# First stage of a vision-transformer kernel reordered: eight embed pieces, norm rows spread by a product, k ahead of q

## The reference

```
x = einsum('bchpwq,dcpq->bhwd', patches, conv_w)      # contraction over 32*8*8 = 2048
x = x.reshape(b, 256, 128) + conv_b
for i in range(2):
    y = _ln(x, ln1_g[i], ln1_b[i])                    # (x - mean) * rsqrt(var + eps) * g + b
    q, k, v = split(y @ qkv_w[i])                     # 8 heads of 64
    q = softmax(q, axis=-1) * scale                   # over a head's 64 columns
    k = softmax(k, axis=-2)                           # over the 256 tokens
    ctx = einsum('bhnd,bhne->bhde', k, v)
    x = x + einsum('bhnd,bhde->bhne', q, ctx) ... @ out_w[i] + out_b[i]
    ...                                               # layernorm, gelu network
```

## Time and profile before

| | |
|---|---|
| median of 3 runs | 131.5 us (131.13 to 131.67) |
| the profiled execution | 131.33 us, of which its span is 129.5 us |
| busy share of the span | PE 92%, PEld 80%, DVE 59%, ACT 50%, POOL 38% |
| DMA | 12.18 MB, nearly all in the first 34 us |
| granted TensorE clock | 1.000 over the span |

### The profile page before, as it was taken

How to read it: one execution, slowest core, us unless ns; L and a number is a source line. 1 busy time by engine, 2 the same in 40 slices (tenths; PEclk the granted TensorE clock), 3 DMA queues, 4 the chain that set the end, 5 groups by cost and what they waited for, 6 DMA issues and landing times.

```text
span 129.5 us, 2185 instructions
## 1 busy us (share of the span) xinstructions
PE 118.7 (92%) x820; PEld 103.5 (80%) x820; DVE 76.2 (59%) x239; ACT 64.3 (50%) x153; POOL 48.7 (38%) x60
## 2 busy tenths in 40 slices
PE   6999959999999999898999999669889988999991
PEld 6999958986987889796876989658578777998991
DVE  6000284897677945669999876347678478065002
ACT  3000153835397395467773649733772835423520
POOL 0000024034797575416759356086409123022000
PEclk9999999999999999999999999999999999999999
DMA  4999899999100000000000000000000000000101
GB/s 109 364 424 418 244 432 384 339 416 407 74 0 0 0 3 0 5 0 0 0 0 0 5 0 3 0 0 0 8 0 0 0 0 0 5 0 0 61 0 61
DMA packets 3884, 12.18 MB, mean 94 GB/s; under 512 B 441, under 2 KB 1817, under 8 KB 3618
## 3 DMA queue, kind: packets, MB, share of 16 engines
q1 hardware_dynamic: 3874, 12.05, 24.8%
HBM read 11.65 MB, written 0.39 MB: 93 GB/s over the span
## 4 chain that ended last, share of the span: by engine, by line
PE 65%; DVE 9%; DMA 9%; ACT 8%; SPq 3%; issue 3%; POOL 2%; DVEq 0%; ACTq 0%; POOLq 0%
DMA norm_rows_sb<-in_norm_rows 9%; PE bank L499 6%; PE bank L375 5%; PE bank L394 5%; PE bank L413 4%; PE bank L319 4%; PE bank L388 3%; PE bank L382 3%; PE bank L340 3%; PE bank L352 3%; SPq L261 3%; PE bank L365 3%; PE bank L485 2%; PE bank L401 2%; PE bank L370 2%
## 5 line engine op out<-in xcount | busy, mean ns | idle before, releaser
L1787 POOL TENSOR_TENSOR rstd<-mv,minus_half 128x2 f32<-128x2 f32 x14 | 10.0, 714 | 39.5 <-DVE mv L934 39.1
L1805 POOL TENSOR_TENSOR qn<-q,rqsum 128x512 f32<-128x512 f32 x8 | 8.3, 1044 | 12.7 <-DVE rqsum L994 12.7
L1566 ACT ACTIVATE patches_sb<-bank,fcb 128x256 f32<-128x256 f32 x12 | 5.1, 471 | 10.5 <-PE bank L496 10.5
L1525 ACT ACTIVATE kexp<-bank,nkmax 128x256 f32<-128x256 f32 x16 | 7.4, 470 | 5.7 <-DVE nkmax L974 5.7
L413 PE MATMUL bank<-restw,hid 128*128 128x128 f32 x64 | 8.8, 281 | 1.0 <-ACT hid L1540 1.0
L394 PEld LDWEIGHTS bank<-cw,qT 128*128 128x128 f32 x64 | 8.1, 191 | 1.7 <-issue 1.0
L499 PE MATMUL bank<-projw,patches_sb 128*128 128x192 f32 x48 | 9.4, 331 | 0.0
L394 PE MATMUL bank<-cw,qT 128*128 128x128 f32 x64 | 9.0, 285 | 0.1
L413 PEld LDWEIGHTS bank<-restw,hid 128*128 128x128 f32 x64 | 7.8, 191 | 1.6 <-ACT hid L1540 1.4
L319 PE MATMUL bank<-embed_sb 128*128 128x128 f32 x64 | 8.5, 288 | 0.0
L319 PEld LDWEIGHTS bank<-embed_sb 128*128 128x128 f32 x64 | 8.1, 200 | 0.3 <-DMA embed_sb<-in_embed 0.2
(11 more groups left out here) (168 smaller groups left out, 341.4 us busy)
## 6 DMA issues: line engine op xcount, KB each, us to landing
embed_sb<-in_embed SPq DMA_DIRECT2D x3, 768.0 KB, 6.9
patches_sb<-in_patches SPq DMA_DIRECT2D x2, 1024.0 KB, 12.5
restw<-in_rest_w SPq DMA_DIRECT2D x2, 768.0 KB, 16.7
qkvw<-in_qkv_w SPq DMA_DIRECT2D x3, 256.0 KB, 11.7
qkvw<-in_qkv_w SPq DMA_DIRECT2D x1, 768.0 KB, 16.5
fcw<-in_fc_w SPq DMA_DIRECT2D x1, 768.0 KB, 18.4
embed_sb<-in_embed SPq DMA_DIRECT2D x1, 576.0 KB, 4.1
aqkvw<-in_aqkv_w SPq DMA_DIRECT2D x1, 576.0 KB, 12.8
```

The costliest lines, as they stand in the source:

```text
L1525: return nc.scalar.activation(kexp[:, c, :], K_BANK[s][c // 2][:, (c % 2) * TOKENS:(c % 2 + 1) * TOKENS], ACT.Exp, bias=nkmax[i][:, c:c + ...
L1787: return nc.gpsimd.tensor_tensor(rstd[i][:], mv[i][:, :, 1], minus_half[:], ALU.pow)
L1805: return nc.gpsimd.tensor_tensor(qn[:, t, :].rearrange("p (h d) -> p h d", h=HEADS), q[:, t, :].rearrange("p (h d) -> p h d", h=HEADS), rq ...
```

## The change

- The embedding of image 0 is loaded in eight pieces (1, 3, then six of 2 chunks) instead of five; image 1's in three (4, 4 and 8 chunks) instead of two.
- The two DMAs for the convolution bias and for the broadcast norm rows of layer 0 are gone. One row of 384 numbers (bias, gain, offset) is loaded second in the queue, into a corner of `ktok` that is not in use yet. PE spreads gain and offset over 128 partitions by a product with one row of ones (`first_norm_rows`), ACT copies the result to `norm_rows_sb[0]`.
- The bias products of both images move from the end of their sums to behind the first chunks; the last chunk closes the sum (`conv_last`). Two warm-up products ahead of the third piece go.
- On PE the k products go ahead of the q products; image 1's chunks 4 and 5 stand between the k products, 6 and 7 behind the q products.
- The low part of the query weights moves from DVE to POOL. DVE takes both means ahead of the centring, and the maxima of k ahead of those of q.
- ACT's two roundings of `aqkvw` move behind the exponentials of k and q, the second one behind the copies of the mixing masks.
- The loads that follow are issued in another order.

The diff, cut to its core:

```diff
-CONV_AT = (0, 1, 4, 8, 12, KCONV)
+CONV_AT = (0, 1, 4, 6, 8, 10, 12, 14, KCONV)
+PATCH_AT = (0, 4, 8, KCONV)
...
+        first_row_sb = ktok[0:1, 0, 0:D + GROW]
...
-            load_embed(0, 1, "embed0")
-            load_embed(1, 4, "embed1")
-            load_embed(4, 8, "embed2")
-            load(convb_sb[:], convb, "cb")
-            load_embed(8, 12, "embed3")
-            load_embed(12, 16, "embed4")
-            load_patches(0, 8, "patches1a")
-            load(norm_rows_sb[0][:], norm_rows0.to_broadcast([P, GROW]), "rg")
+            load_embed(0)
+            load(first_row_sb, first_row, "first_row")
+            for n in range(1, len(CONV_AT) - 1):
+                load_embed(n)
+            load_patches(0)
             load(qkvw[0][:, INNER:2 * INNER], qkv_w[0][:, INNER:2 * INNER], "qkv0k")
             load(small_sb[:], small, "small")
             load(qkvw[0][:, 0:INNER], qkv_w[0][:, 0:INNER], "qkv0q")
+            load_patches(1)
+            load(mix_sb[:], mix, "mix")
             load(headw[:], head_w, "head")
             load(aqkvw[:], aqkv_w, "aqkv")
-            load_patches(8, 16, "patches1b")
+            load_patches(2)
...
+            def first_norm_rows():
+                return nc.tensor.matmul(FIRST_ROWS_BANK[:, 0:GROW], ones[0:1, 0:P], first_row_sb[:, D:D + GROW],
+                                        start=True, stop=True)
...
             conv(1, 0, 2)
+            conv_bias(1)
             conv(1, 2, 4)
-            conv(1, 4, 6)
             pe.wait_ge(y_ready, 2)
             pe.wait_ge(loaded["small"], 16)
             turn(TURN1_BANK[0], y[0]).then_inc(y_turned, 1)
-            conv(1, 6, 8)
...
-            q_high(0, 0)
             k_high(0, 1)
-            q_low(0, 0).then_inc(q_done, 1)
+            k_low(0, 1).then_inc(k_done, 1)
+            pe.wait_ge(loaded_patches[1], 16)
+            conv(1, 4, 6)
             k_high(0, 2)
-            k_low(0, 1).then_inc(k_done, 1)
-            q_high(0, 1)
-            q_low(0, 1).then_inc(q_done, 1)
             k_low(0, 2).then_inc(k_done, 1)
             k_high(0, 3)
             k_low(0, 3).then_inc(k_done, 1)
-            pe.wait_ge(loaded["patches1b"], 16)
+            pe.wait_ge(query_weight_low0, 1)
+            q_high(0, 0)
+            q_low(0, 0).then_inc(q_done, 1)
+            q_high(0, 1)
+            q_low(0, 1).then_inc(q_done, 1)
+            conv(1, 6, 8)
+            pe.wait_ge(loaded_patches[2], 16)
             conv(1, 8, 10)
...
+            act.wait_ge(first_rows_done, 1)
+            evict(norm_rows_sb[0][:], FIRST_ROWS_BANK[:, 0:GROW]).then_inc(first_rows_ready, 1)
             act.wait_ge(moments_done, 1)
             evict(x[0][:, 0, :], CONV_BANK[0][0][:, 0:D]).then_inc(x_ready, 1)
```

More of the change, by code:

```diff
@@ L53, with build @@
 GROW = 2 * D
-CONV_AT = (0, 1, 4, 8, 12, KCONV)
-CONV_PIECES = len(CONV_AT) - 1
-def build(nc, small, convb, norm_rows0, norm_rows1, embed0, patches1, qkv_w, rest_w, rows, mix, fc_w, proj_w,
+CONV_AT = (0, 1, 4, 6, 8, 10, 12, 14, KCONV)
+PATCH_AT = (0, 4, 8, KCONV)
+def build(nc, small, first_row, norm_rows1, embed0, patches1, qkv_w, rest_w, rows, mix, fc_w, proj_w,
           head_w, aqkv_w, aout_w, out):
@@ L213, in build @@
         loaded = {n: sem(f"loaded_{n}") for n in (
-            "aout", "aqkv", "cb", "embed0", "embed1", "embed2", "embed3", "embed4", "fc", "head",
-            "mix", "patches1a", "patches1b", "proj", "qkv0k", "qkv0q", "qkv1", "rest0", "rest1",
-            "rg", "rows", "small", "v0")}
+            "aout", "aqkv", "first_row", "fc", "head",
+            "mix", "proj", "qkv0k", "qkv0q", "qkv1", "rest0", "rest1",
+            "rows", "small", "v0")}
         aqkv_weight_high, attention3_columns, attention3_ready, attention3_turned, attention_done, centred1 = (
@@ L252, in build @@
             sem(n) for n in ("y_ready", "y_turned",))
+        loaded_embed = [sem(f"loaded_embed{n}") for n in range(len(CONV_AT) - 1)]
+        loaded_patches = [sem(f"loaded_patches{n}") for n in range(len(PATCH_AT) - 1)]
+        first_rows_done, first_rows_ready, query_weight_low0 = (
+            sem(n) for n in ("first_rows_done", "first_rows_ready", "query_weight_low0"))
         consts_set = sem("consts_set")
@@ L261, in load, with load_embed, load_patches @@
                 sp.dma_start(dst, src).then_inc(loaded[name], 16)
[L263 to L267 removed]
+            def load_embed(n):
+                at = slice(CONV_AT[n], CONV_AT[n + 1])
+                sp.dma_start(embed_sb[:, at, :], embed0[:, at, :]).then_inc(loaded_embed[n], 16)
+            def load_patches(n):
+                at = slice(PATCH_AT[n], PATCH_AT[n + 1])
+                sp.dma_start(patches1_sb[:, at, :], patches1[:, at, :]).then_inc(loaded_patches[n], 16)
             def store(i, t):
                 sp.dma_start(out[i, :, t, :], outs[i][:, t, :]).then_inc(stored, 16)
[L272 to L279 removed]
+            load_embed(0)
[3 more added lines that the diff above has]
+            load_patches(0)
             load(qkvw[0][:, INNER:2 * INNER], qkv_w[0][:, INNER:2 * INNER], "qkv0k")
@@ L321, in conv, with conv_last, conv_bias @@
                 return mm
-            def conv_bias(i, t):
-                return nc.tensor.matmul(CONV_BANK[i][t][:, 0:D], ones[:, 0:P], convb_sb[:], start=False, stop=True)
+            def conv_last(i, t):
+                c = KCONV - 1
+                left = (embed_sb[:, c, D + t * P:D + (t + 1) * P] if i == 0
+                        else patches1_sb[:, c, t * P:(t + 1) * P])
+                return nc.tensor.matmul(CONV_BANK[i][t][:, 0:D], left, embed_sb[:, c, 0:D], start=False, stop=True)
+            def conv_bias(i):
+                for t in range(TILES):
+                    mm = nc.tensor.matmul(CONV_BANK[i][t][:, 0:D], ones[0:1, 0:P], first_row_sb[:, 0:D],
+                                          start=False, stop=False)
+                return mm
+            def first_norm_rows():
+                return nc.tensor.matmul(FIRST_ROWS_BANK[:, 0:GROW], ones[0:1, 0:P], first_row_sb[:, D:D + GROW],
+                                        start=True, stop=True)
             def turn(dst, src):
@@ L1577, in _ @@
             evict(yT_hi[0][:], TURN1_BANK[0][:, 0:TOKENS]).then_inc(y_high, 1)
-            act.wait_ge(loaded["aqkv"], 16)
-            evict(aqkvw_parts[0][:, 1, :], aqkvw[:, 1, :]).then_inc(aqkv_weight_high, 1)
             act.wait_ge(k_max_ready, 1)
             k_exp(0, 0).then_inc(k_exp_ready, 1)
-            evict(aqkvw_parts[0][:, 0, :], aqkvw[:, 0, :]).then_inc(aqkv_weight_high, 1)
             k_exp(0, 1).then_inc(k_exp_ready, 1)
@@ L1585, in _ @@
             k_exp(0, 2).then_inc(k_exp_ready, 1)
+            k_exp(0, 3).then_inc(k_exp_ready, 1)
             act.wait_ge(q_shifted, 1)
             q_exp(0, 0).then_inc(q_exp_ready, 1)
-            k_exp(0, 3).then_inc(k_exp_ready, 1)
+            act.wait_ge(loaded["aqkv"], 16)
+            evict(aqkvw_parts[0][:, 1, :], aqkvw[:, 1, :]).then_inc(aqkv_weight_high, 1)
             act.wait_ge(moments_done, 3)
@@ L1594, in _ @@
             copy_fc_masks()
+            evict(aqkvw_parts[0][:, 0, :], aqkvw[:, 0, :]).then_inc(aqkv_weight_high, 1)
             act.wait_ge(moments_done, 4)
@@ L1960 @@
     host = {
[L1961 removed]
+        "small": small, "first_row": first_row, "norm_rows1": norm_rows[1], "embed0": embed0, "patches1": patches1,
         "qkv_w": a[T + "qkv_w"], "rest_w": np.stack(rest), "rows": rows,
```

90 lines of the change are left out of this document (41 added, 49 removed).

## The result

| | before | after |
|---|---|---|
| median of the paired runs | 131.57 us (4 runs) | 133.42 us (132.75 to 134.03, 4 runs) |
| ratio, with its 95% interval | | 1.0138 [1.0095, 1.018] |
| profiled execution, its span | 131.33, 129.5 | 132.75, 131.0 |
| mean granted TensorE clock of the single executions | 1.00 in all 70 executions that ran beside the experiments | 1.00 in 5, 0.987 in 4, 0.974 in 1 (10 in all, with r0 below) |

The change makes the kernel slower by 1.4%; the forecast was 131.2 us, its range 130.1 to 132.1. Two things have to be told apart. Five of the ten executions after run at a mean granted clock of 1.00; their median is 132.75 us, some 1.2 us above before. The other five run with a lower clock and take 133.69 to 135.24.

A forecast was written before the change was run, and what follows sets the result against it. The chain was taken to run through the norm-row load, then PE busy from k's first low product. PE's lead, mostly spent ahead of image 1's transpose, leaves 0 to 0.34 us; 0.2 taken, so 131.2 us, range 130.1 to 132.1.

The forecast's parts named there:

- TensorE starts on the second piece: Image 0's embedding: the row load delays the piece's issue, so it lands at 5.75 us, or PE starts at 5.41 as before.
- from there to the transpose of y: Embedding and first layernorm: records, bias and row product end at 13.71 us, transpose at 16.39 instead of 18.18.
- transpose to the first low product of k: Behind y's transpose: `yT_hi` 0.39, `yT_lo` 0.42, 0.11 between and behind; first low product of k at 17.79 us.
- that product to the end of the last `turn_k`: PE's k stretch: 16 more records (1.87 us), two bias products fewer (0.53), so 10.31 us instead of 8.97.
- end of `turn_k` to image 1's transpose: ACT: `aqkvw` rounding ahead of image 1's copy takes 0.58 us, spending PE's lead; transpose at 30.76, or 30.42 if early.
- Rival D: Start of the load queue: the row load comes late and PE waits; almost nothing; chance 0.03 together with C.
- PE idles some 0.9 us behind it: Sign: behind the first transpose of y, PE waits some 0.9 us for the parts of y.
- a gap of half a microsecond ahead of image 1's transpose: Sign: PE idles half a microsecond there, with ACT's copy of image 1's second half right behind `aqkvw_hi`.
- Rival B: POOL's 1.42 us subtraction for `aqkvw` delays image 1's inverse deviation; 132.0 us; decides from a reciprocal at about 26.2; chance 0.11.
- Rival A: PE's lead gets through: early second piece, fewer waits for pieces and k and q products; 0.7 us, 130.6; chance 0.34.
- Rival C: Embedding loads: 384 KB pieces at 255 GB/s starve PE, embedding ends at 15.5 instead of 13.71; 133.1 us; chance 0.03 with D.
- The stretch at 78 GB/s: Loads from 13 to 14 us: probably the norm-row load; without it the weights come a further microsecond earlier.

The follow-up runs named there:

- r0: The changed kernel run once more, with no edit: median 133.32 us, ratio 1.0125 to before.
- e1: Changed kernel with the one-row load issued behind the second embedding piece instead of ahead of it: median 132.46 us, ratio 0.9991 to before.
- e3: Changed kernel with the query weights' low part back on VectorE, behind `yT_lo`: median 132.56 us, ratio 1.0074 to before.
- e6: Changed kernel with GpSimd's query-weight low part waiting until VectorE has made that of the key weights: median 133.17 us, ratio 1.0115 to before.
- e9: Kernel before with only the low part of layer 0's query weights moved to GpSimd: median 131.42 us, ratio 0.9988.
- e4: Changed kernel with image 1's x copied ahead of the second rounding of `aqkvw`: median 132.06 us, ratio 1.0039 to before.
- e8: Changed kernel with row load third, query low part on VectorE, x copied before the rounding, image 0's embedding in five pieces: 130.93 us, ratio 0.9957 to before.
- e2: Changed kernel with image 0's embedding in five pieces again, row load still second: median 134.73 us, ratio 1.0116 to before.
- e10: Changed kernel with query low part on VectorE, x copied before the rounding, norm rows by DMA again, no row product: 131.21 us, ratio 0.9963 to before.

## Why the prediction was wrong

The prediction's steps up to image 1's transpose, each a length between two rows:

| step | before | predicted | after |
|---|---|---|---|
| TensorE starts on the second piece | 5.41 | 5.75 | 6.63 |
| from there to the transpose of y | 12.77 | 10.64 | 10.62 |
| transpose to the first low product of k | 1.53 | 1.40 | 2.01 |
| that product to the end of the last `turn_k` | 8.97 | 10.31 | 10.24 |
| end of `turn_k` to image 1's transpose | 2.08 | 2.66 | 2.63 |
| image 1's transpose | 30.76 | 30.76 | 32.13 |

Three of the five steps came out within 0.07 us; two missed by 0.88 and 0.61, which, less 0.12 by which the other three came out shorter, makes up the whole 1.37.

**The second piece (0.88 us), the step that failed first.** The prediction took the landing time of before, 4.1 us, as fixed and moved only the issue: "So the piece lands at 1.65 + 4.1 = 5.75". The issue did move, to 1.55. But the landing took 5.0, and e1 shows that the row ahead of the piece does it. The same 255 GB/s were read as a queue without a backlog, from which I concluded that only a late issue could count. The bound from below was given (5.41); one from above was missing. Rival D looked at the row itself and called it "almost nothing"; what the row does to the load behind it was no case of mine. How a load of 1.5 KB holds the next one for a microsecond is not shown by these runs.

**VectorE's subtraction (0.61 us), a step that had no cost at all.** The prediction goes from the transpose of y to the first low product by `yT_hi` (0.39), `yT_lo` (0.42) and 0.11 between and behind them. VectorE's subtraction for the key weights, which stands ahead of `yT_lo`, is no term of that sum, and the move of the query weights' subtraction to GpSimd is not mentioned. In the trace `yT_hi` ends at 18.12 and `yT_lo` starts at 18.80, behind the subtraction of 1.76 us. e3, e6 and e9 show why it takes so long. The Trainium skill has the rule: "SBUF — State Buffer", section "🔬 SBUF: two separate sides", says that a VectorE operation with two SBUF inputs and a GpSimd operation that reads SBUF need the same pair of ports, that the first one holds it for its whole instruction and that the other stands still meanwhile. By that rule VectorE, at 17.11, waits for the end of GpSimd's row at 16.89 + 1.44 = 18.33; adding 0.65 gives an end at 18.98, an estimate. The trace shows 17.11 + 1.76 = 18.87, and e6 bears out the part on SBUF inputs. It was the rule that spoke against this change.

**The clock (0.67 us of the median), which no step had.** The profiled execution was predicted and compared at a clock of 1.00, as the rows of before give it everywhere. The prediction named both pauses, "PE idles some 0.9 us behind it" and "a gap of half a microsecond ahead of image 1's transpose", and priced them as time without work only. Half of the executions pay for them again: 133.42 is the median over both kinds, 132.75 that at full clock.

**What was right.** The sum from the second piece to the transpose of y (12.77 us down to 10.64; measured 10.62), though its parts met by luck: the 12 records, the bias and the row product with the idle time among them took 2.61 (predicted 2.34), the last 48 records 5.44 (5.62), the layernorm 2.57 (2.68). PE's additional records between k and `turn_k`. The rounding on ACT: the copy of x stands right behind it, the pause is 0.49 us, and the step came out 0.03 off; e4 shows what it is worth. Rival B did not come: the reciprocal starts at 26.48, past the 26.2 from which B was to decide, but that sum left the variance at 28.7; it came late as well, the subtraction ends at 29.17, and `rstd` at 29.90 waits for the variance. What looks like a small case of the same exclusion is `xg`: 0.35 us, it takes 0.79 beside `aqkvw_lo`. Rival A's lead is lost in the two steps above, and e8 shows no gain from the pieces. Rival C fell with e2 and e8, and in the trace after the queue moves 410 GB/s between 8 and 11 us, where it carries little but the 384 KB pieces. The argument against C had misread its row: between 16.9 and 18.2 most of what before moves is the 576 KB load of `aqkvw` (73 of 132 packets, 336 of 582 KB) and the beginning of image 1's second megabyte of patches, not weights of 128 and 256 KB.

**The stretch at 78 GB/s.** That the norm-row load causes it is borne out: 62 of the 73 packets that start in the stretch are of 1 KB, one row of 256 numbers each. It agrees with the trace after, where the load is gone and the same stretch moves 390, and with e10, where it is back and the stretch moves 208. In before this cost little, since the centring waited for the rows in any case; in e10 the loads behind it are late for the rounding of the weights.

## What to carry to other kernels

A DMA put ahead of another is priced by when the other lands, not by the time of its own issue; on a start that waits for the first large load, even a row of 1.5 KB is better put behind that load. When work moves from VectorE to GpSimd, list what VectorE runs at that moment with two inputs in SBUF, and which of the two starts first: that decides who pays. A new pause of TensorE is to be costed with the clock behind it, over many executions and not from one profile: here the pause ahead of image 1's transpose costs some 0.56 us as idle time (e4) and, in over half of the executions that have it, a microsecond or more by the clock. Undoing three of the edits turned a loss of 1.4% into a gain of 0.6%.
